# Vision tower with mixture of experts on one core: residual rows normalised on VectorE, transposes in another order, two splits and one product moved

## The chip, the cores and the metric

One core of a Trainium2 chip runs the whole kernel. The metric is the device time of one execution in microseconds (us), the median of several. The engines are called as the profile calls them: PE is the matrix engine TensorE, PEld its weight loads, DVE is VectorE, ACT is ScalarE, POOL is GpSimd, SP is SyncE, which here issues transfers only.

## What is computed

A tokenizer, one attention layer and one expert layer, cut to what matters here:

```python
h = tokenizer(x)                                # (64, 5, 256): 4 windows' rows and a class row
h = concatenate([cls_tok, h], axis=1)           # 6 tokens for each of 64 images
h = h + attention(layernorm(h))                 # 16 heads, causal, 6 tokens
m = layernorm(h)                                # "mid": the normalised residual
p, i = top_k(softmax(m @ gate_w), 2)            # the router, 8 experts
y_e = (silu(m @ gate_e) * (m @ up_e)) @ down_e  # 8 experts of width 512
out = h + sum over the two picked experts of p * y_e
```

## The kernel before, in words

The 384 rows (6 tokens of 64 images) stand as three row tiles of 128, numbered 0, 1 and 2, each of two tokens. The order of work is written out by hand for each engine: every engine has its own list of calls, runs it in order, and meets the others by semaphores. `wait_full` and `wait_copied` wait until a PSUM bank is filled or drained for a named use.

Values that go into an exact product are split: a high half in fp32r is made by ACT (names with `_hi`), the low half is the difference of the value and the high half, made by DVE or POOL (names with `_lo`). PE then takes three products of halves.

The stretch that the change touches lies between the attention and the first expert:

- DVE computes scores and softmax weights in three blocks of tokens (`attention_products`, `att_dots`, `att_scores`, `att_weights`; blocks in the order 0, 2, 1, ACT making the exponentials in `attention_exp`). POOL and DVE multiply weights with values (`values`, `token_values`, line 485). `pool_values` and `dve_values` count these products.
- PE turns each block's context (`turn_context`, line 881), ACT copies it (`context_copy`, line 1348), PE adds the output projection to the residual in PSUM (`out_proj`, line 890). Row tile 0 needs block 0, tile 2 blocks 0 and 2, tile 1 block 1.
- For each row tile, DVE takes the moments of the PSUM row (`residual_moments`, lines 1678 to 1685), POOL the reciprocal root by `pow` (`reciprocal_root`, line 1515). For tiles 0 and 1 POOL then multiplies mean and root with -1 (`negative_mean`, line 1521) and ACT normalises (`mid_normalise`, line 1219); for tile 2 DVE normalises (`normalise`, line 1692).
- PE turns the normalised tile (`turn_mid`, line 604), ACT makes the high half (`experts_input_hi`, line 1354), DVE the low half (`experts_input_lo`, line 1957), and PE computes router logits (`router`, line 904: six matrix products a tile). `keep_clock` (line 911) is idle work on PE: two passes of 256 columns a call.
- ACT copies the residual (`residual_copy`) and makes high halves of the normalised rows (`token_rows_hi`); POOL copies rows (`second_rows`, line 1599) and makes their low halves (`token_rows_lo`, line 1579).
- Then PE runs expert 0 for all rows in four quarters (`gate_up`, line 982; ACT `silu`, DVE `hidden`, line 2075), while DVE computes ranks, counts and destinations (the route chain, lines 2045 to 2125), which POOL uses to scatter rows to DRAM (`scatter`, line 1603). Expert 0's input weights are split in quarters by `weights_hi` and `weights_lo` (line 1573), those of the first expert tile by `tile_weights_hi` and `tile_weights_lo` (line 1963, line 1362).
- The remaining seven experts run over 11 tiles of 128 gathered rows (`tile_gate_up`, line 1053; `hidden_turn`, line 1062; `tile_out`, line 1071; `give_back`, line 1084). The first two are gathered by PE, the others are read back from DRAM after the scatter (SP waits for `scattered`, then issues four reads, then the weights of tiles 3 and on) and turned by `rows_turn` (line 1038). ACT makes the high half of the tile's weights in the same list in which it does the silu.

Of the kernel before, what the change touches and what calls it, by code (L numbers as in the profile page):

```python
# [26 lines left out]
C = 256  # L27
# [27 lines left out]
VSTEPS = 5  # L55
REST = KCH[-1][1]
# [3 lines left out]
BLOCKS = [(0, 3), (3, 5), (5, 6)]  # L60
# [15 lines left out]
SLOT_TILES = SPARSE + SPILL  # L76
# [34 lines left out]
NORMED = ["red0", "class", "red1", "in2", "mid2"]  # L111
ACT_NORMED = ["in0", "in1", "mid0", "mid1"]
# [28 lines left out]
def tower_kernel(nc, xa, xb, conv_w, tok_w, att_w, consts, biases, rows, ffn_w, out):  # L141
    ctx = ExitStack()
    with ctx:
# [358 lines left out]
        def _(sp):  # L502
# [25 lines left out]
            def tile_a(s):  # L528
                if s == 1:
                    sp.wait_ge(pool_values, BLOCKS[0][1] + 2)  # L530
                    sp.wait_ge(dve_values, 2)
                if s == 2:
                    sp.wait_ge(a_split, FQ)
                if s >= RING:
                    sp.wait_ge(tile_a_split, FQ * (s - RING + 1))
                sp.dma_start(a_ring[ring(s)].rearrange("p q n -> p (q n)"), expert_of(s)[:, 0:FQ * FFN_A]).then_inc(tile_a_in[s % RING], 16)
# [34 lines left out]
        def _(pe):  # L571
# [303 lines left out]
            def turn_context(k, b):  # L875

                i0, i1 = BLOCKS[k]
                wait_free(pe, b, f"ctx{k}")
                for n, t in enumerate([t for t in CTX_ORDER if i0 <= t < i1]):
                    for j in range(t + 1):  # L880
                        mm = pe.matmul(bank[b][:, n * P:(n + 1) * P], pv[:, pv_at[t] + j, :], ident, start=(j == 0), stop=(j == t))
                mm.then_inc(filled[b], 1)

            def out_proj(j, copied):
                b = ROW_BANK[j]
                for cb, name in copied:
                    wait_copied(pe, cb, name)
                n = CTX_ORDER.index(TOKENS[j][0])
                for half in range(2):
                    mm = pe.matmul(bank[b][:, 0:C], ctxT[:, half, n:n + 2, :].rearrange("p t b -> p (t b)"), wp[:, half, :],  # L890
                                   start=False, stop=(half == 1))
                mm.then_inc(filled[b], 1)
# [15 lines left out]
            def keep_clock(b, n):  # L908

                for _ in range(n):  # L910
                    pe.matmul(bank[b][:, 0:C], ident, wp[:, 0, :], start=True, stop=True)
# [42 lines left out]
            turn_context(2, 1)  # L954
            out_proj(2, [(3, "ctx0"), (1, "ctx2")])
            pe.wait_ge(pool_values, BLOCKS[0][1] + 2)
            pe.wait_ge(dve_values, 2)
            turn_mid(0, 3)
            turn_context(1, 4)
            turn_mid(2, 1)  # L960
            out_proj(1, [(4, "ctx1")])
# [4 lines left out]
            keep_clock(0, 4)  # L966
            turn_mid(1, 4)
            keep_clock(0, 2)
# [140 lines left out]
            for s in range(SLOT_TILES):  # L1109
                tile_gate_up(s)  # L1110
                if s == 0:
                    down(0, 7)
                if s == 1:
                    pe.wait_ge(rows_split, GATHERED)
                    down(1, 2)
                if GATHERED < s + 1 < SLOT_TILES:
                    rows_turn(s + 1)
                if s:
                    tile_out(s - 1)
                if s > 1:  # L1120
                    give_back(s - 2)
                if s + 1 == GATHERED:
                    rows_turn(s + 1)
                hidden_turn(s)
# [7 lines left out]
        def _(act):  # L1132
# [90 lines left out]

            def mid_normalise(j):
                normalise(midn[:, j, :], bank[ROW_BANK[j]][:, 0:C], f"mid{j}").then_inc(act_normed, 1)
# [160 lines left out]
            ins.then_inc(gexp_done, 1)  # L1386
            h_copy(1)
# [8 lines left out]
            weights_hi(3)  # L1396
# [8 lines left out]
            mid_normalise(0)  # L1405
# [3 lines left out]
            context_copy(1, 4)  # L1409
            experts_input_hi(2, 1)  # L1410
            residual_copy(2)
            token_rows_hi(2)
            mid_normalise(1)
            experts_input_hi(1, 4)
# [72 lines left out]
        def _(pool):  # L1487
# [150 lines left out]
            residual(2)  # L1638
            pool.wait_ge(att_step[0], ATT)
# [7 lines left out]
            negative_mean("mid0")  # L1647
            pool.tensor_copy(xrow[:, :, :, ROW_TOKEN], spread(token_of[:, :], 2, PICKS)).then_inc(rows_ready, 1)
            weights_lo(3)
            reciprocal_root("mid2", 1)  # L1650
            pool.memset(hidf[:, :, 0:FIRST], 0.0).then_inc(hid_zero, 1)
# [4 lines left out]
            reciprocal_root("mid1", 1)  # L1656
            negative_mean("mid1")
# [15 lines left out]
        def _(dve):  # L1673
# [92 lines left out]
            def row_moments(j):  # L1766
                dve.wait_ge(h_full, j + 1)
                moments(f"in{j}", [bank[ROW_BANK[j]][:, 0:C]])

# [261 lines left out]
            wait_rstd(dve, "mid0")  # L2031
            tile_weights_lo(0, 0)
            tile_weights_lo(0, 1)
            residual_moments(2)
            experts_input_lo(0, 3)
            normalise("mid2", [bank[ROW_BANK[2]][:, 0:C]], [midn[:, 2, :]])
            experts_input_lo(2, 1)
            residual_moments(1)
            wait_rstd(dve, "mid1")
            tile_weights_lo(0, 2)  # L2040
            tile_weights_lo(0, 3)
            experts_input_lo(1, 4)
# [48 lines left out]
            dve.tensor_tensor(slot[:, :, :], counts[:, 0:RT, :], spread(near_first[:, :], 1, RT), ALU.add).then_inc(route_step, 1)  # L2091
            dve.wait_ge(route_step, 15)
# [9 lines left out]
            hidden(1)  # L2102
# [155 lines left out]
```

## Time and profile before

| | |
|---|---|
| median of 3 runs | 213.6 us (213.53 to 214.21) |
| the profiled execution, its own time | 213.47 us |
| its span in the profile | 211.7 us |
| PE busy | 194.5 us, 92% |
| DVE, ACT, POOL busy | 66%, 51%, 38% |
| granted TensorE clock, mean | 0.995 |

The span is what the profile records, from the first to the last event; 1.8 us of the execution's own time lie outside it. The chain that ended last is PE for 66%, DVE for 17%.

### The profile page before, as it was taken

Reading aid. Unit: us, or ns where it says so; the run is one execution under the profiler, and the core shown is the slowest. Engines: PE = TensorE matmul, PEld = TensorE weight load, DVE = VectorE, ACT = ScalarE, POOL = GpSimd, SP = SyncE. Lnnn points to the kernel's source line nnn. Section 1 sums busy time; section 2 is a strip of 40 time slices with the busy share of each in tenths; the row PEclk is TensorE's granted clock in tenths of the full one; section 3 lists DMA queues with packets and bytes.
Section 4 is the critical chain, followed back from the end, with each engine's and each line's share of the span. In section 5 each row is a group of like instructions: output and inputs, shape, how many; then the busy total and the mean of one; then the engine's idle time right before and its main releaser. Section 6 shows DMA issues by size and latency. Waiting matters only on the chain.

```text
span 211.7 us, 3444 instructions
## 1 busy us (share of the span) xinstructions
PE 194.5 (92%) x1142; PEld 169.7 (80%) x1142; DVE 140.1 (66%) x338; ACT 108.7 (51%) x235; POOL 80.6 (38%) x108
## 2 busy tenths in 40 slices
PE   1999999999999998898967999999999999999991
PEld 1899999998897885876956878988788888888871
DVE  1664976385999998755897448646588677666411
ACT  3575294555327355434831434244487676777320
POOL 4027165274474030366059644485032211122220
PEclk9999999999999999999999999999999999999997
DMA  6999997000491000000004800124999988843003
GB/s 214 339 383 400 303 317 213 3 0 0 138 413 49 0 3 0 0 0 2 3 0 136 362 0 2 37 91 131 374 384 369 326 302 315 301 134 101 0 0 74
DMA packets 10189, 32.90 MB, mean 155 GB/s; under 512 B 1190, under 2 KB 5628, under 8 KB 8508
## 3 DMA queue, kind: packets, MB, share of 16 engines
q1 hardware_dynamic: 8120, 29.53, 39.5%
q10 hardware_dynamic: 1764, 2.37, 3.4%
q0 software_dynamic: 288, 0.79, 1.0%
q8 instruction: 9, 0.15, 0.3%
q14 instruction: 8, 0.07, 0.1%
HBM read 30.05 MB, written 2.64 MB: 154 GB/s over the span
## 4 chain that ended last, share of the span: by engine, by line
PE 66%; DVE 17%; issue 4%; ACT 3%; DMA 3%; POOL 3%; SPq 2%; ACTq 0%; DVEq 0%
PE bank L1053 14%; PE bank L580 10%; PE bank L1071 9%; PE bank L657 6%; PE bank L1084 4%; PE bank L982 3%; DMA raw<-xb 3%; PE bank L992 2%; PE bank L1062 2%; PE bank L604 2%; DVE stats L1678 2%; DVE split L1802 2%; DVE kv_rows L1732 1%; PE bank L722 1%; SPq L468 1%
## 5 line engine op out<-in xcount | busy, mean ns | idle before, releaser
L1053 PE MATMUL bank<-split 128*128 128x512 f32 x132 | 33.2, 400 | 0.5 <-DVE split L2136 0.5
L1611 POOL TENSOR_SCALAR split<-token_row,window 128x384 fp32r<-128x384 f32 x11 | 15.4, 1398 | 46.3 <-PE bank L1084 46.3
L580 PE MATMUL bank<-split 128*128 128x256 f32 (+1 forms) x225 | 28.3, 285 | 0.2 <-DVE split L1804 0.2
L1053 PEld LDWEIGHTS bank<-split 128*128 128x128 f32 x132 | 24.0, 188 | 5.5 <-DVE split L2136 0.7
L580 PEld LDWEIGHTS bank<-split 128*128 128x128 f32 (+1 forms) x225 | 27.5, 191 | 0.5 <-DVE split L1804 0.3
L657 PE MATMUL bank<-split 128*128 128x512 f32 x108 | 26.5, 397 | 0.0
L1515 POOL TENSOR_TENSOR rstd<-veps,mhalf 128x1 f32<-128x1 f32 (+2 forms) x17 | 14.2, 835 | 27.9 <-DVE veps L1685 27.6
L657 PEld LDWEIGHTS bank<-split 128*128 128x128 f32 x108 | 19.8, 188 | 3.9
L1963 DVE TENSOR_TENSOR split<-raw,split 128x512 fp32r<-128x512 f32 x28 | 18.4, 697 | 6.6 <-ACT split L1362 5.2
L1535 POOL TENSOR_TENSOR window<-window,pe_rows 128x256 f32<-128x256 f32 x14 | 14.5, 1034 | 8.6 <-ACT pe_rows L1140 8.0
L1362 ACT CAST split<-raw 128x512 fp32r<-128x512 f32 x28 | 16.5, 620 | 1.9 <-DMA raw<-ffn_w 1.9
L1202 ACT ACTIVATE kv_rows<-bank,rstd 128x512 f32<-128x512 f32 x18 | 12.1, 689 | 10.1 <-PE bank L657 9.3
L1140 ACT COPY pe_rows<-bank 128x256 f32<-128x256 f32 x18 | 6.5, 373 | 18.7 <-PE bank L580 17.6
L2145 DVE TENSOR_TENSOR kv_rows<-bank,kv_rows 128x512 f32<-128x512 f32 x11 | 7.6, 690 | 11.8 <-PE bank L1053 9.1
L595 PE MATMUL bank<-split 128*128 128x256 f32 (+1 forms) x45 | 8.6, 369 | 5.1 <-ACT split L1154 5.1
L1963 DVE TENSOR_TENSOR split<-kv_rows,split 128x512 fp32r<-128x512 f32 x16 | 11.1, 735 | 2.0 <-ACT split L1362 1.9
L595 PEld LDWEIGHTS bank<-split 128*128 128x128 f32 (+1 forms) x45 | 8.1, 275 | 5.4 <-ACT split L1154 5.4
L1084 PE MATMUL bank<-split 128*128 128x256 f32 x66 | 11.5, 309 | 0.7 <-DVE split L2151 0.7
L1802 DVE TENSOR_TENSOR split<-raw,split 128x1536 fp32r<-128x1536 f32 x5 | 8.8, 1754 | 4.9 <-ACT split L1163 4.9
L1678 DVE BATCH_NORM_STATS2 stats<-pe_rows 128x6 f32<-128x256 f32 x18 | 6.5, 414 | 8.1 <-ACT pe_rows L1140 8.1
L1084 PEld LDWEIGHTS bank<-split 128*128 128x128 f32 x66 | 9.2, 189 | 1.7 <-DVE split L2151 1.2
L1362 ACT CAST split<-kv_rows 128x512 fp32r<-128x512 f32 x16 | 9.5, 620 | 0.5 <-DMA kv_rows<-ffn_w 0.5
(274 smaller groups left out, 400.4 us busy)
## 6 DMA issues: line engine op xcount, KB each, us to landing
raw<-ffn_w SPq DMA_DIRECT2D x7, 1024.0 KB, 7.5
kv_rows<-ffn_w SPq DMA_DIRECT2D x4, 1024.0 KB, 7.2
raw<-xa SPq DMA_DIRECT2D x5, 768.0 KB
raw<-ffn_w SPq DMA_DIRECT2D x7, 512.0 KB, 8.5
kv_rows<-ffn_w SPq DMA_DIRECT2D x4, 512.0 KB, 6.8
tok<-tok_w SPq DMA_DIRECT2D x1, 1536.0 KB, 12.6
raw<-ffn_w SPq DMA_DIRECT2D x1, 1536.0 KB, 6.4
expert_rows<-zero_row SPq DMA_DIRECT2D x1, 1419.0 KB, 12.9
```

The lines of the kernel that those rows point to most:

```text
L580: mm = pe.matmul(bank[b][:, 0:C], xs[0:n, g % 2, px, a:a + P], cws[0:n, pw, k, :], start=(k == 0 and m == 0), stop=(k == len(KCH) - 1 and ...
L595: mm = pe.matmul(bank[j][:, 0:C], xs[0:n, 0, px, a:a + P], cws[0:n, pw, k, :], start=(k == 0 and m == 0), stop=(k == len(KCH) - 1 and m == 2))
L657: mm = pe.matmul(bank[b][:, :], lns[:, g % 2, px, a:a + P], wkvs[:, pw, aw:aw + 2 * C], start=(c == 0 and m == 0), stop=(c == CC - 1 and m ...
L1053: mm = pe.matmul(bank[half][:, :], xst[:, s % 2, px, c * P:(c + 1) * P], tile_aws[s % 2][:, piece, pw, :], start=(c == 0 and m == 0), stop ...
L1071: mm = pe.matmul(bank[6][:, 0:C], hcols[s % 2][:, q * P:(q + 1) * P], b_ring[ring(s)][:, q, :], start=(q == 0), stop=(q == FQ - 1))
L1084: mm = pe.matmul(bank[SUM_BANK[j]][:, 0:C], back[:, s % 2, j * P:(j + 1) * P], eo[:, s % 2, px, :], start=(s == 0 and px == HI), stop=(s = ...
L1362: act.copy(tile_aws[s % 2][:, piece, HI, :].rearrange("p (q n) -> p q n", q=FQ), a_ring[ring(s)][:, :, piece * P:(piece + 1) * P]).then_in ...
L1515: pool.tensor_tensor(rstd[0:parts, k, 0:n], veps[0:parts, k, 0:n], mhalf[0:parts, 0:n], ALU.pow).then_inc(rstd_done, 1)
L1535: pool.tensor_tensor(redsum[:, wt, :], pe_rows[:, wt, 0, :] if n == 1 else redsum[:, wt, :], pe_rows[:, wt, n, :], ALU.add).then_inc(sum_s ...
L1611: pool.tensor_scalar(back[:, s % 2, :], token_row[:, :], xr[:, s % ROW_RING, ROW_TOKEN:ROW_TOKEN + 1], None, ALU.is_equal).then_inc(back_d ...
L1802: dve.tensor_tensor(xs[:, g % 2, LO, 0:n], x_raw[:, g % RAW_X, 0:4, :].rearrange("p k n -> p (k n)"), xs[:, g % 2, HI, 0:n].bitcast(F32), ...
L1963: dve.tensor_tensor(tile_aws[s % 2][:, piece, LO, :].rearrange("p (q n) -> p q n", q=FQ), a_ring[ring(s)][:, :, piece * P:(piece + 1) * P] ...
```

## The change

DVE normalises all three residual rows, ACT none; POOL computes the three roots without the negative means. PE turns the last block's context right after the one before it, projects both, and turns all three normalised tiles before any router product. The split of expert 0's last quarter moves ahead on ACT and POOL. A quarter of the first tile's weights goes to another place on DVE, and one `hidden` product goes ahead in the route chain. The third tile's rows are turned before the output of the first tile.

```diff
-NORMED = ["red0", "class", "red1", "in2", "mid2"]
-ACT_NORMED = ["in0", "in1", "mid0", "mid1"]
+NORMED = ["red0", "class", "red1", "in2", "mid0", "mid2", "mid1"]
+ACT_NORMED = ["in0", "in1"]
...
             turn_context(2, 1)
+            pe.wait_ge(pool_values, BLOCKS[0][1] + 2)
+            pe.wait_ge(dve_values, DVE_VALUES)
+            turn_context(1, 4)
             out_proj(2, [(3, "ctx0"), (1, "ctx2")])
-            pe.wait_ge(pool_values, BLOCKS[0][1] + 2)
-            pe.wait_ge(dve_values, 2)
+            out_proj(1, [(4, "ctx1")])
             turn_mid(0, 3)
-            turn_context(1, 4)
+            keep_clock(0, 2)
             turn_mid(2, 1)
-            out_proj(1, [(4, "ctx1")])
+            keep_clock(0, 1)
+            turn_mid(1, 4)
             pe.wait_ge(gate_split, 1)
             wait_free(pe, 2, "router")
             router(0, 3)
             router(2, 1)
-            keep_clock(0, 4)
-            turn_mid(1, 4)
-            keep_clock(0, 2)
             router(1, 4).then_inc(filled[2], 1)
...
# PE, the tile loop
-                if GATHERED < s + 1 < SLOT_TILES:
+                if GATHERED <= s + 1 < SLOT_TILES:
                     rows_turn(s + 1)
...
-                if s + 1 == GATHERED:
-                    rows_turn(s + 1)
                 hidden_turn(s)
...
# ACT
+            weights_hi(3)
             h_copy(1)
             in_normalise(1)
...
             attention_exp(0)
-            weights_hi(3)
             tile_weights_hi(0, 0)
...
             context_copy(2, 1)
-            mid_normalise(0)
+            context_copy(1, 4)
             experts_input_hi(0, 3)
             residual_copy(0)
             token_rows_hi(0)
-            context_copy(1, 4)
             experts_input_hi(2, 1)
+            experts_input_hi(1, 4)
             residual_copy(2)
             token_rows_hi(2)
-            mid_normalise(1)
-            experts_input_hi(1, 4)
             residual_copy(1)
             token_rows_hi(1)
...
# POOL
             residual(2)
+            weights_lo(3)
             pool.wait_ge(att_step[0], ATT)
...
             reciprocal_root("mid0", 1)
-            negative_mean("mid0")
             pool.tensor_copy(xrow[:, :, :, ROW_TOKEN], spread(token_of[:, :], 2, PICKS)).then_inc(rows_ready, 1)
-            weights_lo(3)
             reciprocal_root("mid2", 1)
+            reciprocal_root("mid1", 1)
             pool.memset(hidf[:, :, 0:FIRST], 0.0).then_inc(hid_zero, 1)
             second_rows(0)
             token_rows_lo(0)
             second_rows(2)
             token_rows_lo(2)
-            reciprocal_root("mid1", 1)
-            negative_mean("mid1")
             second_rows(1)
             token_rows_lo(1)
...
# DVE
+            def mid_normalise(j):
+                normalise(f"mid{j}", [bank[ROW_BANK[j]][:, 0:C]], [midn[:, j, :]])
...
             residual_moments(0)
-            wait_rstd(dve, "mid0")
+            mid_normalise(0)
             tile_weights_lo(0, 0)
             tile_weights_lo(0, 1)
+            tile_weights_lo(0, 2)
             residual_moments(2)
+            residual_moments(1)
+            mid_normalise(2)
+            mid_normalise(1)
             experts_input_lo(0, 3)
-            normalise("mid2", [bank[ROW_BANK[2]][:, 0:C]], [midn[:, 2, :]])
             experts_input_lo(2, 1)
-            residual_moments(1)
-            wait_rstd(dve, "mid1")
-            tile_weights_lo(0, 2)
+            experts_input_lo(1, 4)
             tile_weights_lo(0, 3)
-            experts_input_lo(1, 4)
...
             dve.tensor_tensor(slot[:, :, :], counts[:, 0:RT, :], spread(near_first[:, :], 1, RT), ALU.add).then_inc(route_step, 1)
+            hidden(1)
             dve.wait_ge(route_step, 15)
...
             dve.tensor_tensor(slot1[:, :, :], slot[:, :, :], fmask, ALU.mult).then_inc(route_step, 1)
-            hidden(1)
```

## Rows read from the trace of the kernel before

**Rows 1.** Busy time by engine, clock, DMA, from the last value product to the router's end
```profile
core 0: us, PE busy (x) PEld busy (x) DVE busy (x) ACT busy (x) POOL busy (x), PEclk, DMA share, GB/s
113.00:125.60 12.60, 10.53 (x69) 8.60 (x67) 5.96 (x15) 4.52 (x13) 8.98 (x15) 1.00 0.54 209
```

**Rows 2.** The chain that ended last, 113 to 129 us: start, duration, piece
```profile
113.19 0.56 POOL rstd L1515
...
120.02 0.44 DVE stats L1678
...
120.94 0.56 POOL rstd L1515
121.59 1.29 POOL nmr L1521
...
124.00 0.38 ACT split L1354
...
124.40 0.44 DVE split L1957
...
124.88 0.83 PE bank L904 x6
125.71 3.70 PE bank L982 x24
```

**Rows 3.** PE in order of time: start, duration of the run, count, idle before
```profile
112.07 1.50 PE L881 MATMUL bank<-con,window 128*128 128x128 f32 x12
...
116.22 2.17 PE L881 MATMUL bank<-con,window 128*128 128x128 f32 x18
118.23 0.38 PE L604 MATMUL bank<-con,pe_rows 128*128 128x128 f32 x2
118.85 1.13 PE L890 MATMUL bank<-att,pe_rows 128*128 128x256 f32 x4 [0.24 <-ACT pe_rows L1348]
119.63 1.58 PE L904 MATMUL bank<-gsplit,split 128*128 128x8 f32 x12
121.08 1.97 PE L911 MATMUL bank<-att,con 128*128 128x256 f32 x8
```

**Rows 4.** DVE in order of time, from 93 to 122 us
```profile
93.38 0.36 DVE L1994 TENSOR_TENSOR gsc<-gsc,gm 128x32 f32<-128x32 f32 x1
...
100.36 0.54 DVE L1692 TENSOR_SCALAR pe_rows<-bank,mv,rstd 128x256 f32<-128x256 f32 x1 [0.74 <-POOL rstd L1515]
101.36 0.76 DVE L494 TENSOR_TENSOR vprod<-kv_rows 128x576 f32<-128x576 f32 x1 [0.46 <-ACT kv_rows L1337]
...
102.95 0.23 DVE L1929 SCALAR_TENSOR_TENSOR kv_rows<-kv_rows,con 128x72 f32<-128x72 f32 x1
...
107.78 0.83 DVE L1929 SCALAR_TENSOR_TENSOR kv_rows<-kv_rows,con 128x80 f32<-128x80 f32 x1
...
121.53 1.29 DVE L1963 TENSOR_TENSOR split<-raw,split 128x512 fp32r<-128x512 f32 x2 [0.67 <-POOL rstd L1515]
```

**Rows 5.** POOL in order of time, from 92 to 109 us
```profile
92.41 3.74 POOL L1573 TENSOR_TENSOR split<-raw,split 128x512 fp32r<-128x512 f32 x3
...
100.22 0.74 POOL L1617 TENSOR_TENSOR pe_rows<-pe_rows,bias 128x256 f32<-128x256 f32 x1
107.10 1.78 POOL L485 TENSOR_TENSOR window<-kv_rows 128x256 f32<-128x256 f32 x3 [6.14 <-DVE kv_rows L1949]
```

**Rows 6.** ACT in order of time, its wait before `h_copy(1)`
```profile
96.31 0.37 ACT L1242 COPY pe_rows<-bank 128x256 f32<-128x256 f32 x1 [1.79 <-DVE stats L1678]
```

**Rows 7.** PE behind the router: expert 0's last quarter, the third tile
```profile
132.07 2.02 PE L982 MATMUL bank<-split 128*128 128x322 f32 x12 [0.35 <-DVE vprod L2075]
...
150.17 3.03 PE L1053 MATMUL bank<-split 128*128 128x512 f32 x12 [0.48 <-DVE split L2136]
...
155.69 0.60 PE L1062 MATMUL bank<-con,kv_rows 128*128 128x128 f32 x4
```

**Rows 8.** ACT and DVE in order of time, around the weights of tile 3
```profile
153.44 0.62 ACT L1362 CAST split<-raw 128x512 fp32r<-128x512 f32 x1 [1.90 <-DMA raw<-ffn_w]
...
154.70 0.68 DVE L2145 TENSOR_TENSOR kv_rows<-bank,kv_rows 128x512 f32<-128x512 f32 x1
```

More of the change, by code:

```diff
@@ L55 @@
 VSTEPS = 5
+DVE_VALUES = 2
 REST = KCH[-1][1]
@@ L530, in tile_a @@
                     sp.wait_ge(pool_values, BLOCKS[0][1] + 2)
-                    sp.wait_ge(dve_values, 2)
+                    sp.wait_ge(dve_values, DVE_VALUES)
                 if s == 2:
@@ L1222, in in_normalise @@
                 normalise(inn[:, j, :], bank[ROW_BANK[j]][:, 0:C], f"in{j}").then_inc(act_normed, 1)
-            def mid_normalise(j):
-                normalise(midn[:, j, :], bank[ROW_BANK[j]][:, 0:C], f"mid{j}").then_inc(act_normed, 1)
             def residual_copy(j):
```

## The prediction, as recorded before the run

> **What bounds the kernel now.** I read the page first (PE busy 92%, so only stretches where PE waits can give time), then the chain that ended last, then the four engines' lists around the edit, and last the transfers. The busy shares say little here. In the stretch from 113.0 to 125.6 us PE is busy for 10.53 us of 12.60 [rows 1], but part of that is idle work and router products that nobody waits for yet. The chain tells what the stretch is: it goes through the root of tile 0, a 1.29 us negative mean, a normalise on ACT, the last context, its projection, moments, root, a negative mean again, normalise, turn, split, and the last six router products, which end at 125.71 [rows 2]. From there on PE runs nearly without a gap to the end, so what the router's end gains or loses is gained or lost at the end, as long as the scatter and the tiles' weights move with it. They do: both wait for the route chain on DVE, which starts from the router's logits.
>
> In what follows all times are on the clock of the kernel before. "Shift" is what is added to them.
>
> **Part 1, POOL's subtraction ahead of the attention: +0.7.** `weights_lo(3)` goes to where POOL stood idle for 6.14 us before 107.10 [rows 5]. It starts when the residual addition ends (100.22 + 0.74 = 100.96) and takes 3.74 / 3 = 1.25 us [rows 5], so to 102.2. The slot is free, but not the neighbour: DVE's first attention product wants to start at 101.36 and reads two operands from SBUF [rows 4]. Three rows show what happens to such an instruction when POOL is inside one of its own. The 80-element operation at 107.78 took 0.83 us where the same one with 72 elements took 0.23 [rows 4], and POOL ran value products from 107.10 to 108.88 [rows 5]. The 32-element subtraction at 93.38 took 0.36 and ended at 93.74 [rows 4], just behind the end of POOL's first subtraction (92.41 + 1.25 = 93.66) [rows 5]. The other way round, POOL's negative mean of one column took 1.29 us [rows 2] under DVE's pair of subtractions from 121.53 to 122.82 [rows 4], and ended at 122.88. So I take it that who comes second waits for the end of the other's instruction: the product starts near 102.05 and not at 101.36, which is +0.7. From there to the last value product DVE has no gap, so the shift reaches all of it. Bounds: 0, if the two only overlap, and 102.2 - 101.36 = 0.85.
>
> This is where a rule of the Trainium skill speaks against the change. "SBUF — State Buffer", section "Who interferes with whom", says that a VectorE instruction with two SBUF inputs and a GpSimd instruction that reads SBUF exclude each other, and the first one holds the port to its end. The three rows agree; by the rule the cost is the 0.7 of above, and without it this term would be nothing.
>
> The same split's ACT half, 0.6 us, goes into ACT's wait before `h_copy(1)`, 1.79 us at that place [rows 6], and costs nothing; if that cover were gone it would cost its 0.6.
>
> **Part 2, from the last value product to the router's end: -3.6.** I lay out the new order from 113.13, when POOL's last value product ends, just ahead of tile 0's root at 113.19 [rows 2].
>
> PE: `turn_context(2)` issues from 112.07; 18 products issue in 118.23 - 116.22 = 2.01, so 0.112 each [rows 3], and 12 are out at 113.4. `turn_context(1)` follows at 113.43 (before: 116.22, behind the turn of tile 0) and is out at 115.44, full at 115.60. `out_proj(2)` starts at 115.44, ends after 1.13 at 116.57, and issues in 119.63 - 118.85 = 0.78 [rows 3]. Its context copy was long done. `out_proj(1)` needs ACT's copy of block 1 (115.62 + 0.38 = 116.0, by the 256-column copies [rows 2]), starts at 116.22 and ends at 117.35. Before, it ended at 118.85 + 1.13 = 119.98 [rows 3]: this half of the gain, 2.6 us, comes from the order on PE alone.
>
> DVE: moments of tile 0 end as before, the root ends at 113.75 [rows 2]. DVE normalises tile 0 from 113.78 for 0.54 (the PSUM normalise of `in2` [rows 4]), to 114.32. Three weight subtractions of 1.29 / 2 = 0.645 [rows 4] last to 116.26. Moments of tile 2 start at 116.59. From the start of moments to the start of the root it is 120.94 - 120.02 = 0.92 [rows 2], so its root runs 117.5 to 118.07, under the moments of tile 1. Those start at 117.40, are done at 118.24, and the root of tile 1 runs 118.32 to 118.88. DVE normalises tile 2 from 118.24 to 118.78 and tile 1 from 118.90 to 119.44. Here the negative mean (1.29) and the handing on to ACT are gone from between root and turn. Then the low half of tile 0, 0.44, to 119.8.
>
> PE again: turn of tile 0 at 117.0, two `keep_clock`, turn of tile 2 at 118.8, one `keep_clock` (0.45 by 8 instructions in 1.97 [rows 3]), turn of tile 1 at 119.47, full at 119.9. High half on ACT 0.38, low half on DVE 0.44 [rows 2]: ready at 120.7. Router products issue at (121.08 - 119.63) / 2 = 0.725 a tile [rows 3]. Tile 0 starts at 119.82, behind its low half, tile 2 at 120.54, tile 1 at 121.27, later than its halves need; end 122.1. So the router's end goes from 125.71 to 122.10: -3.6. The new limit is PE's own 18 products in a row. Bounds: -4.0 if the low half of tile 0 were there when the last turn is out, and -2.8 if each of the three DVE-POOL-DVE handings costs another 0.25, since none of the chain's rows shows two normalises in a row.
>
> `tile_weights_lo(0, 3)` ends near 121.4 and lies under the router. The three `second_rows` and `token_rows_lo` pairs come after the roots now, and so later against the router.
>
> **Part 3, POOL's last low half in the route chain: +0.3.** ACT's queue now has the high half of the turned tile 1 ahead of two residual copies and two row casts (0.38 each [rows 2], overlapping by a tenth), so the cast of tile 1's rows is done at about 121.4. POOL then has two subtractions of the 128x256 kind (0.74 [rows 5]) and a copy to do and ends about 122.9, where before it was done when the router was. DVE's second route operation that reads two SBUF operands wants to start at 122.6: by the same three rows it waits 0.3. PE has 0.15 of room there, the scatter has none. Bounds: 0, and one whole instruction of 0.74.
>
> **Part 4, behind the router: -0.3.** `hidden(1)` ahead in the chain takes away PE's stop before the last quarter, 0.35 in the row and up to 0.5 by the issue [rows 7]. The rows turned before the first tile's output take away the 0.48 before tile 2 [rows 7]. Together PE would stand 1.0 us nearer to the scatter. But ACT waits 1.90 us for the transfer of tile 3's weights, until 153.44, with the silu of tile 2 behind that cast in its list, and DVE's product of tile 2 ends at 154.70 + 0.68 = 155.38 [rows 8]. That transfer hangs on the scatter and so on the route chain. PE turned the product at 155.69 [rows 7]. So only 0.3 of the 1.0 arrives: what is late next is the weights of tile 3. Bounds: 0 and -1.0.
>
> **Not on the path.** The third tile's weight transfer is issued some 2.5 us earlier, since `a_split` no longer ends it; the tile is used at 150.17 [rows 7], so nothing waits. The other waits on SP move with the value products.
>
> **Sum.** +0.7 - 3.6 + 0.3 - 0.3 = -2.9. The profiled execution's own time is 213.47 (span 211.7 and 1.8 around it), so 210.6; the median of the runs lies 0.1 above it, so 210.7 for the median.
>
> **Rivals.**
> 1. No wait at the port (terms 1 and 3 nothing): -3.9, 209.7. For it: no row shows precisely this pair, and POOL's spans are rough. Against it: three places where the ends coincide within 0.1 us.
> 2. The scatter side is late: the weights of tile 3 share the DMA engines with those of tiles 2 and 4, whose requests come closer behind them now that PE is ahead, and part 2's handings cost their upper bound. Then term 4 is +0.3 and term 2 -2.8: -1.5 in all, 212.1. For it: the 1.90 us wait. Against it: bytes and order of the requests are the same.
> 3. Slower: the TensorE clock. PE's wait for the attention becomes 0.7 longer, and between 118 and 119 it waits again, with fewer real products and three calls of idle work where there were six. If the granted clock, 1.00 throughout [rows 1], fell to its lower level of 1.2 GHz, each us of PE work at it would cost another. The loss begins from 2.9 us of work; five would give 215.7. Against it: it was 1.00 although PE stood for 2.07 of the 12.60 us of that row.
> 4. The router's end doesn't move the end, since something else sets the start of the tiles: within 0.3% of before. I see no such wait but the one of part 4.
>
> **How the numbers follow.** My forecast (210.2 to 211.3) has 0.57, rival 1 0.15, rival 2 0.17, rival 3 0.05, rival 4 0.06. A measurement of this kernel can tell 0.3% (0.6 us) from no change. Faster than that: 0.57 + 0.15 + 0.17 = 0.89; within: 0.06; slower: 0.05. The range has to take in rivals 1 and 2 with the bounds of term 4: 209.3 to 212.2.
>
> **What would show it.** In the changed kernel's profile: the first attention product at line 494 starts 0.7 late or takes 1.4 us instead of 0.76, and all DVE work to the last value product lies 0.7 later; POOL's last value product ends near 113.85; no 1.29 us POOL instruction stands after it; the last router product ends near 122.8; one small DVE operation in the route chain takes 0.5 instead of 0.18; PE has no idle time before the last quarter and before tile 2, and a new one before it turns tile 2's product. The forecast is wrong if the clock row shows less than 1.00, if PE waits between the turns for longer than 0.7, or if the distance from the router's end to the last product, 207.7 - 125.7 = 82.0 us before, grows.

## The result, and the profile after

The changed kernel takes 211.31 us, median of 4 runs (210.47 to 211.83), against 213.56 for the kernel before on the same chip (4 runs, 213.41 to 214.21): ratio 0.9862, 95% interval 0.9816 to 0.9909. The two medians alone give 0.9895, and 12 later runs of the same kernel (experiment 9) give 0.9890, inside that interval. The forecast was 210.7 with 209.3 to 212.2, so the median is 0.6 above it and inside the range, at the upper edge of the forecast's own 210.2 to 211.3. Ratios, here and below, leave out executions more than 1.5% above the fastest of the same kernel, 7 in all (2 of 6 in experiment 1, 1 each in 2, 3 and 7, 2 of 12 in 9), while the medians take in all of them. The profiled execution takes 211.25 (span 209.4) and stood at 213.47 (span 211.7) before.

First the page of the changed kernel: span, busy times, granted clock.

```profile
span 209.4 us, 3428 instructions
PE 193.1 (92%) x1136; PEld 169.5 (81%) x1136; DVE 141.7 (68%) x340; ACT 108.0 (52%) x233; POOL 77.0 (37%) x106
PEclk9999999999999999999999979999999999999999
```

The busy shares say as little as before. What is new is one 7 in the clock row, in the slice just behind the router. Next the chain that ended last, from the attention to the first expert; it answers to [rows 2].

```profile
116.92 0.88 PE bank L891 x4
117.83 0.44 DVE stats L1670
...
119.53 0.46 DVE pe_rows L1684
120.03 0.44 PE bank L605 x2
...
121.22 2.13 PE bank L905 x18
123.35 5.21 PE bank L983 x24
128.58 0.32 PE bank L1004 x3
128.91 3.69 PE bank L983 x24
```

ACT's two normalises and POOL's two negative means, which this chain went through before, are gone; DVE's normalise stands in their place. The router is one block of 18 products that ends at 123.35, where it ended at 125.71. Behind it stand the four quarters of expert 0, 12 products each, in two blocks of 24. The blocks should look alike, since their instructions have the same shape, but the first takes 5.21 us and the second 3.69. The table of the same stretch by windows says why.

```profile
core 0: us, PE busy (x) PEld busy (x) DVE busy (x) ACT busy (x) POOL busy (x), PEclk, DMA share, GB/s
113.00:118.00 5.00, 5.00 (x39) 4.82 (x38) 3.84 (x9) 0.64 (x2) 2.16 (x3) 1.00 0.51 164
118.00:121.00 3.00, 2.70 (x16) 1.82 (x14) 2.62 (x10) 1.32 (x4) 1.95 (x5) 1.00 1.00 415
121.00:123.00 2.00, 2.00 (x19) 1.82 (x17) 1.42 (x4) 1.53 (x5) 1.49 (x3) 1.00 0.66 279
123.00:124.00 1.00, 1.00 (x7) 1.00 (x7) 0.54 (x3) 0.00 (x0) 1.00 (x3) 0.61 0.08 16
124.00:126.00 2.00, 2.00 (x9) 2.00 (x8) 1.78 (x7) 1.59 (x3) 0.31 (x1) 0.50 0.00 0
126.00:127.00 1.00, 1.00 (x6) 1.00 (x6) 0.76 (x5) 0.35 (x1) 0.21 (x1) 0.68 0.00 0
127.00:130.00 3.00, 3.00 (x23) 3.00 (x22) 1.55 (x8) 0.50 (x2) 1.00 (x3) 1.00 0.00 0
```

TensorE's clock goes from 1.00 to 0.50, which is 1.2 GHz in place of 2.4, and is back at 1.00 by 127. PE had not stood still ahead of it: 5.00 busy of 5.00, 2.70 of 3.00, 2.00 of 2.00. Two rows of DVE and two of POOL in order of time answer to [rows 4, 5].

```profile
102.04 1.42 DVE L495 TENSOR_TENSOR vprod<-kv_rows 128x576 f32<-128x576 f32 x1 [0.46 <-ACT kv_rows L1333]
...
123.82 0.53 DVE L2044 TENSOR_TENSOR lsub<-lg,rmax 128x24 f32<-128x24 f32 x1
```

```profile
101.57 1.28 POOL L1567 TENSOR_TENSOR split<-raw,split 128x512 fp32r<-128x512 f32 x1
...
123.58 0.73 POOL L1573 TENSOR_TENSOR split<-pe_rows,split 128x256 fp32r<-128x256 f32 x1
```

The product now takes 1.42 us where it took 0.76, and ends at 103.46. Taken back by 0.76 that is 102.70, about where POOL's subtraction ends (102.85): so I read the recorded start as the moment at which the product wanted to run, and its duration as holding the wait. Behind the router the route chain's `lsub` takes 0.53 while POOL is in its last subtraction (to 124.31).

Last, PE and ACT behind the router, answering to [rows 7, 8].

```profile
136.08 3.09 PE L1054 MATMUL bank<-split 128*128 128x512 f32 x12
...
147.95 3.00 PE L1054 MATMUL bank<-split 128*128 128x512 f32 x12
```

```profile
150.29 0.62 ACT L1358 CAST split<-raw 128x512 fp32r<-128x512 f32 x1 [1.48 <-PE bank L1054]
```

No idle time stands before PE's tile 2 any more, and ACT's cast of tile 3's weights, which waited 1.90 us for the transfer before, waits for PE in this execution. The second profile of the same kernel (experiment 9) has it waiting for the transfer again, 1.84 us, and there too PE loses nothing by it.

One wait between DVE and PE matters for what follows. The route chain needs the rank products that PE computes behind the first block of 24. Its step `place` waits for them, in the kernel before and in the changed one:

```profile
129.79 0.17 DVE L2085 SCALAR_TENSOR_TENSOR place<-bank,mask 128x6 f32<-128x6 f32 x1 [0.24 <-PE bank L1003]
```

```profile
128.94 0.16 DVE L2080 SCALAR_TENSOR_TENSOR place<-bank,mask 128x6 f32<-128x6 f32 x1 [1.41 <-PE bank L1004]
```

In the changed kernel `place` starts 5.59 us behind the router's end, and 4.08 us behind it in experiment 11, where the first block takes 3.84 us. So the time that the clock costs in the first block is passed on to the route chain, and with it to the scatter.

**Where the time went.** Cut at four marks, the two profiles compare so. "Conv" is the start of PE's second group of convolution products, ahead of which nothing was changed; A runs from there to the end of the router, B on to tile 0's gate/up products, C to tile 2's, D to the end of PE's last product. "Quarters" is the part of B that the first two quarters of expert 0 take.

| us | conv at | A | B | quarters | C | D | conv to last product |
|---|---|---|---|---|---|---|---|
| before | 14.67 | 111.04 | 11.86 | 3.84 | 12.60 | 57.52 | 193.02 |
| changed | 15.32 | 108.03 | 12.73 | 5.36 | 11.87 | 57.51 | 190.14 |
| difference | +0.65 | -3.01 | +0.87 | +1.52 | -0.73 | -0.01 | -2.88 |

The start of the convolution is put apart from the change: it lies between 14.35 and 16.52 over the 14 profiles of this study, without order. Timed runs scatter by more than a us, it seems for this and for the clock (both vary from profile to profile), so in what follows each kernel has both: its profile from "conv" to the last product, and its ratio to the kernel before.

### The profile page after: what moved, and what is told of

Read it like the earlier page. It is cut to its first block, busy times and chain, and to the rows that moved or that the text cites. A ratio compares the mean times of both kernels' runs of the same rounds, so it can differ in the third digit from the quotient of the medians.

```text
span 209.4 us, 3428 instructions
## 1 busy us (share of the span) xinstructions
PE 193.1 (92%) x1136; PEld 169.5 (81%) x1136; DVE 141.7 (68%) x340; ACT 108.0 (52%) x233; POOL 77.0 (37%) x106
## 4 chain that ended last, share of the span: by engine, by line
PE 71%; DVE 16%; issue 3%; DMA 3%; ACT 3%; SPq 2%; POOL 1%; ACTq 0%; DVEq 0%
PE bank L1054 15%; PE bank L581 10%; PE bank L1072 9%; PE bank L658 6%; PE bank L983 4%; PE bank L1085 4%; DMA raw<-xb 3%; PE bank L993 3%; PE bank L882 2%; PE bank L1063 2%; DVE stats L1670 2%; PE bank L605 2%; DVE split L1797 2%; DVE vprod L495 1%; DVE kv_rows L1724 1%
## 5 line engine op out<-in xcount | busy, mean ns | idle before, releaser
L1605 POOL TENSOR_SCALAR split<-token_row,window 128x384 fp32r<-128x384 f32 x11 | 14.5, 1321 | 46.1 <-PE bank L1085 46.1
```

The source lines that it names most:

```text
L1605: pool.tensor_scalar(back[:, s % 2, :], token_row[:, :], xr[:, s % ROW_RING, ROW_TOKEN:ROW_TOKEN + 1], None, ALU.is_equal).then_inc(back_d ...
```

## The experiments

Two theories of the clock were tested. **A:** it falls because PE's wait before the attention is longer now. **B:** it falls because the router's narrow products (8 columns each) now run in one block of 18, where wide `keep_clock` products, 12 in six calls (8 of them in [rows 3]), lay between the first 12 and the last 6. The other experiments price the terms of the sum.

**1. The product without POOL's subtraction.** This kernel leaves out the low-half subtraction of the last weight quarter and writes zeros in its place.

```diff
-                weights_lo(3)
+                pool.wait_ge(a_hi, FQ)
+                pool.memset(aws[:, FQ - 1, LO, :].bitcast(F32), 0.0).then_inc(a_split, 1)
```

> The changed kernel, but POOL writes zeros in place of the last quarter's low half (it leaves that subtraction out; POOL reads nothing from SBUF there). Port theory: the first attention product (line 495) takes 0.76 us again instead of 1.42, and the end comes 0.65 us earlier than in the changed kernel, as far as the clock is the same. Rival (the product is long for another reason, such as its operands being written late by ACT): it stays near 1.4 us and the end doesn't move.

DVE and POOL in order of time, in this kernel:

```profile
101.04 0.76 DVE L495 TENSOR_TENSOR vprod<-kv_rows 128x576 f32<-128x576 f32 x1 [0.46 <-ACT kv_rows L1333]
```

```profile
100.56 0.53 POOL L1634 MEMSET split<- 128x512 f32 x1
```

The product is back at 0.76 and A is 0.68 shorter (107.35), so the term is real and its size is that of one wait. The writing of the zeros (100.56 to 101.09) overlaps the product's start (101.04) by only 0.05 us, too little to tell whether it could delay it. The last product of PE does not follow: 191.32 from conv, 1.18 longer than the changed kernel. C is 0.52 longer (12.39; SyncE issues the four row reads in 2.83 us) and D 1.35 (58.86): here tile 3's weights are late. ACT and PE in order of time:

```profile
151.59 0.62 ACT L1358 CAST split<-raw 128x512 fp32r<-128x512 f32 x1 [3.91 <-DMA raw<-ffn_w]
```

```profile
153.59 0.66 PE L1063 MATMUL bank<-con,kv_rows 128*128 128x128 f32 x4 [1.12 <-DVE kv_rows L2141]
```

PE stands 1.12 us before it turns tile 2's product. So the wait that the forecast feared exists, and bites in this execution. Six runs: median 210.88, ratio 0.9777 [0.9726, 0.9827], which rests on four of the six and on a kernel that leaves work out.

**2. PE's wait before the attention filled.**

```diff
-            keep_clock(0, 8)
+            keep_clock(0, 11)
```

> The changed kernel with 11 in place of 8 calls of idle work on PE ahead of the attention, where PE otherwise stands for 1.75 us; the three calls take 1.35 us of that wait and cost nothing. Theory A, the clock falls after the router because PE stood longer before the contexts: it stays at 1.00 from 123 to 127 us and the first two quarters of expert 0 take 3.7 us instead of 5.2, so the end comes 1.5 us earlier. Theory B, it falls because of the 18 narrow router products in a row just ahead: nothing changes, the two quarters take 5.2 again.

PE in order of time, in this kernel:

```profile
104.08 4.91 PE L912 MATMUL bank<-att,con 128*128 128x256 f32 x22
109.44 1.60 PE L882 MATMUL bank<-con,window 128*128 128x128 f32 x12 [0.45 <-POOL window L486]
...
122.38 5.33 PE L983 MATMUL bank<-split 128*128 128x322 f32 x24
```

The wait before the attention is 0.45 in place of 1.75, and the quarters still take 5.33. Theory A falls for this wait. The profile is as long as the changed kernel's (190.13). 211.21, ratio 0.9857 [0.9804, 0.9910].

**3. Wide products between the router's tiles.**

```diff
             router(0, 3)
+            keep_clock(0, 1)
             router(2, 1)
+            keep_clock(0, 1)
             router(1, 4).then_inc(filled[2], 1)
```

> The changed kernel with one call of idle work (two passes of 256 columns, 0.45 us) behind each of the first two row tiles' router products. It delays the router's end by at most 0.9 us. Theory B (18 narrow products in a row bring the clock down): the clock stays at 1.00 and the first two quarters take 3.7 us, net 0.6 us earlier than the changed kernel. Theory A (the wait before the contexts does): the clock falls as before, the quarters take 5.2, and the end is 0.9 later.

PE in order of time, in this kernel:

```profile
121.23 0.68 PE L912 MATMUL bank<-att,con 128*128 128x256 f32 x2
...
123.44 3.83 PE L985 MATMUL bank<-split 128*128 128x322 f32 x24
```

The quarters are back at 3.83, with the clock at 1.00 all through: theory B holds in this profile. It is no free cure, since the two calls put 0.86 into A (108.89 against 108.03). C is 12.22 and not 11.87, with the row reads issued in 2.43 us. The profile comes to 189.88, 0.26 less than the changed kernel where 0.6 was expected, and the runs show no gain: 212.47 (9 runs, 210.38 to 214.35), ratio 0.9907 [0.9869, 0.9945]. The profiled run is the fastest of the nine, and five of the others have a mean clock of 0.991 or less.

**4. The kernel before, with part 4 alone.**

```diff
-                if GATHERED < s + 1 < SLOT_TILES:
+                if GATHERED <= s + 1 < SLOT_TILES:
...
-                if s + 1 == GATHERED:
-                    rows_turn(s + 1)
...
+            hidden(1)
...
-            hidden(1)
```

> The kernel before with part 4 alone: the product of the second quarter ahead in the route chain, and the third tile's rows turned before the first tile's output. My recorded theory: PE comes to tile 2 about 1.0 us earlier, but only 0.3 arrives at the end, since ACT still waits for the weights of tile 3. Rival, from the changed kernel's trace, where ACT no longer waited for that transfer: 1.0 to 1.4 us arrive, all of it.

B is 11.30 and C 12.21 where they were 11.86 and 12.60: 0.56 and 0.39, and D keeps 57.47. The second might be 0.73 but for SyncE, which took 2.41 us to issue the four row reads where it takes 1.75 in the kernels before and after (SyncE's queue in this kernel, in order of time):

```profile
144.75 2.41 SPq L455 DMA_DIRECT2D window<-expert_rows  x4
```

213.36 in 12 runs, ratio 0.9969 [0.9939, 0.9998]; 1.0 us would be 0.9953, and 0.3 us 0.9986, so the runs allow both. The profile shows 192.03 against 193.02, the whole 1.0 of part 4, where 0.3 was in the sum.

**5. POOL's last subtraction in the gap before the root of `in2`.**

```diff
                 residual(1)
+                weights_lo(3)
                 reciprocal_root("in2", 1)
```

> The changed kernel with the same subtraction one place earlier in POOL's list, between the second residual addition and the root of in2, where POOL stands for 1.3 us and DVE works on PSUM operands alone. Port theory: the work costs nothing there, the attention product takes 0.76 us, the root of in2 is at most 0.1 late, and the distance from the second conv group to the router's end is 0.65 shorter than in the changed kernel (108.03 there, so 107.4). Rival (the subtraction delays whatever follows it on POOL): the root of in2 comes 0.6 to 1.3 late and nothing is won.

POOL and DVE in order of time, in this kernel:

```profile
98.84 1.27 POOL L1567 TENSOR_TENSOR split<-raw,split 128x512 fp32r<-128x512 f32 x1
100.22 0.55 POOL L1509 TENSOR_TENSOR rstd<-veps,mhalf 128x1 f32<-128x1 f32 x1
```

```profile
101.88 0.76 DVE L495 TENSOR_TENSOR vprod<-kv_rows 128x576 f32<-128x576 f32 x1 [0.46 <-ACT kv_rows L1333]
```

The subtraction ends before the root is wanted, the product takes 0.76, and A is 107.34, 0.69 less than in the changed kernel. All of the computation is kept. In the profile it is lost again in C (12.59, with the row reads issued in 2.99 us and PE waiting 0.50 us for the rows), and the total stays at 190.12. 210.91, ratio 0.9855 [0.9818, 0.9893].

**6. Tile 3's transfer ahead of the scatter.**

```diff
+                tile_a(3)
                 sp.wait_ge(scattered, ...)
...
-                tile_a(3)
```

> The changed kernel with the transfer of tile 3's gate weights issued ahead of SP's wait for the scatter, not behind the four row reads. If that transfer is what is late next, ACT's wait for it (1.3 to 3.9 us in the profiles so far, 1.9 in the kernel before) and PE's wait for tile 2's product (1.12 us in one profile, none in four) are gone, the runs scatter less and the median falls by 0.3 to 1 us. Rival: the transfer only trades places with others, ACT waits for tile 4's instead, PE gets no time from it.

ACT no longer waits for any transfer there, and the profile stays as it was: D 57.50 and the total 190.10 against 57.51 and 190.14. 210.77, ratio 0.9839 [0.9792, 0.9885]. So in the changed kernel's profile this wait costs PE nothing; that it helps the runs in which the transfer is late, as in experiment 1, is not shown.

**7. The changed kernel with ACT normalising the residual rows again.**

```diff
-NORMED = ["red0", "class", "red1", "in2", "mid0", "mid2", "mid1"]
-ACT_NORMED = ["in0", "in1"]
+NORMED = ["red0", "class", "red1", "in2", "mid2"]
+ACT_NORMED = ["in0", "in1", "mid0", "mid1"]
```

> The changed kernel with one part undone: tiles 0 and 1 are normalised by ACT again, with POOL's negative means, all orders as changed. My sum has PE's order as 2.6 of the 3.6 and the rest from normalising on DVE: root of tile 1, then 0.27 negative mean (DVE has no two-operand SBUF instruction there, so it isn't 1.29), 0.1 handing, 0.56 on ACT, against 0.54 on DVE: the last turn 0.4 later and the router's end 0.4 later. Rival, the change's first words (DVE normalising is what saves the time): 1.3 us or more later.

PE in order of time, before the last turn of this kernel:

```profile
120.53 0.44 PE L605 MATMUL bank<-con,pe_rows 128*128 128x128 f32 x2 [0.50 <-ACT pe_rows L1218]
```

A is 108.44, 0.41 longer. So with the other parts in place the normalise on DVE is worth 0.4 of part 2's 3.7 us, as expected. The clock falls here too (quarters 5.33). C is 12.29, with the row reads issued in 2.67 us, and the profile comes to 191.10, 0.96 more than the changed kernel. 211.64, ratio 0.9894 [0.9853, 0.9936].

**8. Three changes at once:** those of experiments 5 and 6, and one wide call in the router.

```diff
             router(0, 3)
+            keep_clock(0, 1)
             router(2, 1)
```

> The changed kernel with the subtraction in POOL's gap, the transfer of tile 3 ahead of the wait, and one call of idle work (0.45 us) behind the first tile's router products. By the three theories: 0.65 and 0.3 to 1 us won, and 1.5 less 0.4 us where the clock held; median 2 us under the changed kernel's, 209.3 if that is 211.3. If one call isn't enough to hold the clock, the quarters still take 5.2 and it is 0.5 to 1.2 us under.

PE in order of time, in this kernel:

```profile
121.06 1.59 PE L905 MATMUL bank<-gsplit,split 128*128 128x8 f32 x12
122.51 3.84 PE L984 MATMUL bank<-split 128*128 128x322 f32 x24
```

A 107.77 (0.69 less for the subtraction, 0.43 more for the call), B 11.28, C 11.86, D 57.52: 188.43 in all, 1.71 less than the changed kernel. 209.16 in 6 runs (208.28 to 210.77), ratio 0.9792 [0.9750, 0.9834]. The transfer of tile 3 gives nothing here either: C and D are the changed kernel's.

**9 and 10. The changed kernel again, and the kernel before with DVE normalising alone.** The second is the kernel before in which the two normalises of the residual rows stand on DVE and their negative means are left out; the order of all the rest is that of before.

```diff
-NORMED = ["red0", "class", "red1", "in2", "mid2"]
-ACT_NORMED = ["in0", "in1", "mid0", "mid1"]
+NORMED = ["red0", "class", "red1", "in2", "mid0", "mid2", "mid1"]
+ACT_NORMED = ["in0", "in1"]
```

> The changed kernel itself once more, beside the other three on one chip, as their measure. The same picture: product 1.42 us, from the second conv group to the router's end 108.0, quarters at 5.2 where the clock falls. If the weights of tile 3 come late here, from the router's end to the last product is 82.7 or more where the first profile had 82.1.

> The kernel before with one part alone: DVE normalises tiles 0 and 1, no negative means; PE's order, the split and everything else as before. In the last run PE's new order kept all but 0.4 us of the 3.7 without this part. If the two parts save the same waits twice over (either takes most of it alone), this one wins 2.6 us up to the router's end: 1.2 at the turn of tile 0, 1.35 at that of tile 1. Rival, additive shares as in my sum: 1.0 us.

The changed kernel: 211.54 in 12 runs (209.84 to 213.07), ratio 0.9890 [0.9856, 0.9924], profile 190.08, quarters 5.35. DVE normalising alone: 213.76 in 12 runs, ratio 1.0003 [0.9973, 1.0034]; A is 109.94, so 1.10 gained at the router's end, which is the rival's 1.0 and not the 2.6. The whole 1.10 reaches the last product in the profile (191.92), yet the interval of the runs allows no more than 0.6 us. What takes it away in the runs is not known. POOL, DVE and PE of that kernel, in order of time:

```profile
114.38 1.27 POOL L1571 TENSOR_TENSOR split<-raw,split 128x512 fp32r<-128x512 f32 x1
```

```profile
114.77 2.02 DVE L1959 TENSOR_TENSOR split<-raw,split 128x512 fp32r<-128x512 f32 x2
```

```profile
118.80 0.44 PE L604 MATMUL bank<-con,pe_rows 128*128 128x128 f32 x2 [0.91 <-DVE pe_rows L1688]
```

DVE's two weight subtractions take 2.02 where a pair takes 1.29 [rows 4], because POOL is in `weights_lo(3)` at its old place. That 0.7, behind the 0.54 us normalise that DVE now does first, pushes the moments and the normalise of tile 2 back, and PE waits 0.91 for it.

**11. POOL's copy of the last rows behind its last low half.**

```diff
-                second_rows(1)
                 token_rows_lo(1)
                 token_weights()
+                second_rows(1)
```

> The changed kernel with POOL's copy of tile 1's rows behind the token weights, and its low half at once behind that of tile 2. Port theory for the route chain: the low half ends 0.4 us earlier and DVE's second two-operand operation there (lsub) takes at most 0.3 us and not 0.53, the route chain is 0.2 to 0.35 shorter. What it gives at the end depends on who is late behind the router: 0.3 where the scatter is, nothing where PE is. Rival: lsub is long for another reason, 0.53 stays.

DVE, POOL and PE in order of time, in this kernel:

```profile
124.51 0.18 DVE L2044 TENSOR_TENSOR lsub<-lg,rmax 128x24 f32<-128x24 f32 x1
```

```profile
122.98 1.68 POOL L1573 TENSOR_TENSOR split<-pe_rows,split 128x256 fp32r<-128x256 f32 x2 [0.51 <-ACT split L1264]
```

```profile
123.90 3.84 PE L983 MATMUL bank<-split 128*128 128x322 f32 x24
```

`lsub` takes 0.18 and not 0.52, and yet C is 11.87 as in experiment 9 (11.86): the 0.35 on the route chain never reached PE. In experiment 9 it lay under `place`'s 1.42 us wait for PE. No run has the long `lsub` with the clock held; `place` waits 0.25 here, so an estimate from these rows is that 0.1 of the 0.35 would then be left. The surprise is the third row. The router is one block of 18 here too, and the quarters take 3.84: 188.65 in all, 209.80 in 6 runs (209.58 to 211.19), ratio 0.9824 [0.9781, 0.9867], with a mean clock of at least 0.997 in each of the six. The edit touches nothing of PE.

**12. Experiments 8 and 11 together,** with POOL's first window sum also made to wait for its weights' split.

```diff
+                wait_split(pool, 1)
                 window_sum(0)
```

> The changed kernel with the subtraction in POOL's gap, tile 3's transfer ahead, one call of idle work in the router, the copy of tile 1's rows behind, and POOL's first window sum waiting for DVE's split of the second patch group (so that the two cannot meet at 14 us, where the profile of the changed kernel lost 0.5). By the theories 0.65, 0.3 to 1, 1.1, 0 to 0.3 and 0 to 0.5: 2 to 3 us under the changed kernel on the same chip, and less scatter. If the first sum delays the second conv group, it is no better than the version with three fixes.

188.45 in all, quarters 3.84; 210.05 in 6 runs, ratio 0.9813 [0.9770, 0.9857]. It is no better than experiment 8, and in this profile the convolution started at 16.52.

**The best of these** with all of the computation kept is experiment 8, 0.9792 [0.9750, 0.9834]: faster than the kernel before, and its interval lies below that of the changed kernel's 12 runs, 0.9890 [0.9856, 0.9924]. The intervals of experiments 11 and 12 overlap with its own, so that it beats the one moved line of experiment 11 is not shown.

## Why the prediction was right, and where it was not

| term | forecast | measured in the profile | by |
|---|---|---|---|
| Part 1, product behind POOL | +0.7 | +0.67 | 0.76 to 1.42; given back in 1 and 5 |
| Part 2, to the router's end | -3.6 | -3.68 | A, less part 1 |
| Part 3, `lsub` behind POOL | +0.3 | 0 at the end | 0.35 on DVE, under the wait of `place` |
| Part 4, behind the router | -0.3 | -1.30 | B without the clock, C and D |
| clock | not in the sum | +1.43 | 12.73 against 11.30 in B |
| sum | -2.9 | -2.88 | |

The sum is right to a few hundredths by luck. Part 4 gave 1.0 us more than forecast and part 3 cost 0.3 less, and the clock, which the sum left out, took 1.43 back. The prediction's own signs say so: it called itself wrong if the clock row showed less than 1.00, and it shows 0.50, and if the distance from the router's end to the last product grew, and it went from 81.98 to 82.11, although part 4 takes 1.3 out of it. The third sign, PE waiting more than 0.7 us between the turns, did not come (0.30).

**Part 1** went as worked out, mechanism and size. The rule of the Trainium skill named there ("SBUF — State Buffer", "Who interferes with whom") is borne out by it: 0.76 to 1.42 us, and back at 0.76 in experiments 1 and 5.

**Part 2** has the right end, 3.7 against 3.6, and no 1.29 us POOL instruction is left. The forecast put 2.6 of the gain down to PE's order alone and the remaining 1.0 to the normalise on DVE. Experiment 10 has 1.1 at the router's end for the normalise alone, near that share, though the runs can't tell it from nothing (1.0003). Experiment 7 shows that the order and the moved subtraction keep 3.3 without it. So the two shares overlap by 0.7: 1.1 and 3.3 are more than 3.7. With `weights_lo(3)` in its old place DVE's pair of subtractions takes 0.7 longer (experiment 10), which may be that overlap; a run with the normalise and this one move alone is missing. At its new place the subtraction costs 0.67 that it need not, since the gap one root earlier is free (experiment 5).

**Part 3** has the right mechanism (0.53 against 0.18), but its price at the end is nothing. The forecast gave the scatter no room. The route chain has one in `place`'s wait for PE's rank products, 0.24 us in the kernel before and 1.41 in the changed one, where the fallen clock keeps PE late.

**Part 4 is one of the two failing steps:** "so only 0.3 of the 1.0 arrives: what is late next is the weights of tile 3". In neither profile of the changed kernel are they late for PE, and the idle time of PE before tile 2's product, which the prediction expected, is in neither. The whole 1.0 arrives, with 0.3 more because C had 0.73 to give where 0.48 was read from the row and B 0.56 where it was 0.5. The step took one execution's 1.90 us wait [rows 8] for a fixed distance behind the scatter. The profiles have that transfer landing between 5.0 and 7.1 us after its issue, so it binds in some executions: by 1.12 on PE in experiment 1, by nothing in the changed kernel and in experiment 6.

**The clock is the other.** The sum put it at nothing, with "it was 1.00 although PE stood for 2.07 of the 12.60 us of that row" as the reason. Rival 3, which has it, was given 0.05. Of the causes that it names, the longer wait ahead of the attention is ruled out by experiment 2; the wait between the turns, 0.30 us, also stands in experiments 3 and 8, where the clock held; the fewer calls of idle work remain. Its price, each us of work at the lower level costing another, was a little high: the four windows at 0.61, 0.50, 0.50 and 0.68 lack 1.71 us of full clock, and 1.43 is what they cost. Without that the profile would have gained 4.3 us. Experiment 11, the same order with the clock held, shows 4.4 (193.02 to 188.65), and experiment 8 4.6 (188.43), with part 1's 0.69 given back for the 0.43 of the wide call.

The median missed by 0.6, and the profiled execution by the same: 211.25 against 210.6, which is the convolution's later start (0.65) and no part of the change. Of the 12 runs in experiment 9, 9 have a mean clock of 0.992 or less.

**What stays open.** Eight profiles have the changed order on PE and no wide call in the router; the clock fell in 7 and held in experiment 11. It held in all 3 with one or two calls there, and in all 3 with the order of before. So in the profiles the block of narrow products goes with the fall. That it causes it is not shown, for two reasons. What kept the clock up in all six runs of experiment 11, whose PE work is the same, is not known. And the timed runs, of which only the mean clock is on record, do not bear the wide call out as a cure. Every profile with the fall has a mean of 0.992 or less and every one without it 0.994 or more, and by that mark 11 of the 21 runs of experiments 3, 8 and 12 have a fall somewhere, against 34 of 46 without a call (experiment 11 left out) and 7 of 24 in experiments 4 and 10, with the order of before. In experiment 8 its two runs of this kind are its slowest, 210.2 and 210.8. Also open is why SyncE takes 1.75 us to issue the four row reads in some kernels and 2.4 to 3.0 in others.

## What to carry to other kernels

When work is taken off a stretch of PE, look at which idle-work calls lay between its narrow products, and look at the granted clock behind such a block, also where PE is busy throughout. A POOL instruction goes into a gap of DVE's two-operand work and not only into a gap of POOL: here the slot one root earlier was free and the chosen one cost 0.7 us. Before pricing a delay on a side chain, look for the place where that chain waits for the main one. Read a wait for a transfer from more than one execution before it caps a gain, and split a sum that came out right into its terms, since errors of 1 us each can cancel.

## What the hardware showed that was not expected

- The clock fell to 0.50 directly behind 18 products of 8 columns that took 2.14 us, with PE busy 9.70 of the 10.00 us up to 123.00. With a wide call of two products behind the first six it held in 3 of 3 profiles, without one in 1 of 8; the timed runs show no such clear difference.
- The same hold of POOL on DVE shows at the very start, in code that was not changed. DVE's 76x384 subtraction took 1.08 us in the changed kernel and in experiment 5, and 0.55 before; POOL's window sum had begun just ahead of it. DVE and POOL in order of time, in the changed kernel:

```profile
14.18 1.08 DVE L1799 TENSOR_TENSOR split<-raw,split 76x384 fp32r<-76x384 f32 x1
```

```profile
14.06 0.79 POOL L1529 TENSOR_TENSOR window<-pe_rows 128x256 f32<-128x256 f32 x1 [11.31 <-ACT pe_rows L1139]
```

  Which of the two comes first is decided by 0.1 us, so one program gives either: in experiment 9, the same kernel, DVE began at 13.97 and POOL at 14.09, and the subtraction took 0.55. PE waited 1.10 us for this subtraction in the first profile and 0.18 before, which more than covers the 0.65 by which the convolution began later.
- The transfer of tile 3's weights landed 5.0 to 7.1 us after its issue, though the requests around it are the same from kernel to kernel (in 6, 8 and 12 it is only ahead of the scatter).
